# Scores six steps ahead of the weighted latents instead of eight, and a new order of work on every engine

## The chip, the cores and the metric

The kernel runs on one core of one Trainium2 chip. The metric is the device time of one execution in microseconds. A core has five engines that run side by side and synchronise by semaphores: TensorE (PE, matrix products), VectorE (DVE), ScalarE (ACT), GpSimd (POOL) and SyncE (SP), which here issues DMA copies.

## The reference

Input: x of 32 batches x 256 tokens x 128 features, in fp32. Output: x plus an attention term (with its own residual) plus a feed-forward term.

```python
x = L0_attn_x
xn = _layernorm(x)                       # no scale, no bias
# attention, on xn
h = layernorm(xn) * ln_scale + ln_bias
c_q, c_kv = h @ w_down_q.T, h @ w_down_kv.T            # 64 latents each
q, k, v = (c_q @ w_up_q.T), (c_kv @ w_up_k.T), (c_kv @ w_up_v.T)   # 16 heads of 64
q, k = rope(q), rope(k)
attn = softmax(q @ k.T / 8)                            # 256 x 256 per head
att = (attn @ v) @ w_out.T + xn
# feed-forward, on xn
y = square(relu(xn @ W_fc.T)) @ W_proj.T
spikes = 5 steps of a leaky integrator on y, mean of the spikes
return x + att + spikes
```

## The kernel before

**Steps.** The 16 heads of a batch are 8 pairs; one pair of one batch is a step, so there are 256 steps g. The loop body is written for two steps at once (a double step), and a batch b has four of them, q = 0 to 3. Every engine runs the same sequence of double steps, and in each it works on several steps at once, each at another stage. `LEAD` (L27) says how far a stage runs ahead of the last one: at double step g TensorE projects steps g+14 and g+15, POOL finishes the rotation of g+12 and g+13, the scores, maxima, exponentials and transposes are those of g+8 and g+9, and the weighted latents those of g and g+1. The first double step is g = -14 (`FIRST`).

**One step, in order.** `project` (TensorE, L341, L342: four f32r products into the one bank `ps_qk`); `copy_projected` (ACT, L626: raw); `rotate` (DVE, L813: times cosine, which frees `ps_qk` for the next projection); `exchange` (SP, L273: two copies of 128 KB each way swap neighbouring partitions of two steps, `partner`; it waits until POOL is done with the buffer of four steps before, and for raw); `add_rotated` (POOL, L1010 and L1013: times sine, plus); `scores` (TensorE, L353, half the rows of the array for each of two heads); `row_max` (DVE, L818); `exponentials` (ACT, L614: four of them with row sums); `turn` (DVE, L830: 32x32 transposes into `turned`).

**The move.** `move` (SP, L260 to L264) brings the turned weights of a group of four steps into `gathered` by 16 copies of 128 KB. It waits for the last transpose of the group, then for the weighted latents that last read this half of `gathered`. In double step s it is the group whose last step is s + LEAD["scores"] + 1, which falls on q = 1 and q = 3. `weigh_latents` (TensorE, L369, half the columns for each of two heads) waits at the first step of a group for all 16 copies (`moved`). `copy_u` (ACT, L633) takes the result.

**Once per batch.** The sums of the exponentials are inverted (`invert_sums`, DVE L837), split (`split_sums`, POOL), transposed (`transpose_rden`, TensorE L432), broadcast in four chunks (`broadcast_rden`, TensorE L440; `copy_spread`, ACT L639), multiplied in (`normalise_u`, POOL L1054), and `attention_out` (TensorE L474) multiplies by the output weights in four pieces. The latents of batch b+2 are made by `latents` (TensorE L387), `lead_latents` (ACT L670) and `split_latents` (DVE L858), and the first projection of that batch waits for them. `latents_by_token` (L394), `ffn_in` (L410), `relu`, `square`, `ffn_out` (L423), `integrate` (DVE L866, L869), `add_spikes` (L886), `transpose_sum` (L483), `finish` (L897), `moments_of` (DVE L844, L850), `inverse_std` (POOL L1019 to L1028), `normalise` (ACT L655), `residual` (POOL L1036) and `transpose_inputs` (L382) are the rest.

**What sets the order.** The order is written out by hand, in the `step` function of each engine; an engine does what stands there and waits by semaphores. SP's DMA queue is in order too: a copy is issued after those that stand before it. The buffers that tie the engines: one bank for projections, two for score steps (`ps_s`), one for weighted latents (`ps_u`), `ps_b` for sums, broadcasts and attention output, `ps_a` for latents and feed-forward, eight slots of `qk`, two halves of `turned` and of `gathered`.

## Time and profile before

| | us |
|---|---|
| median of 3 runs (1031.68 to 1032.57) | 1032.14 |
| the profiled execution | 1031.75 |
| its span in the trace | 1030.0 |
| PE busy | 990.9 (96%) |
| ACT, DVE, POOL busy | 914.3, 907.0, 895.2 (89, 88, 87%) |
| DMA engines, share of the main queue; bytes of all | 78.8%; 218 MB |

The span runs from the first to the last recorded instruction. A busy PE is one with matmuls in flight; their ends are modelled, so the distance from start to start is what the rows of matmuls are read by. "PEld" is the loading of weights, which lies beside the matmuls. Granted clock 1.00 is the full 2.4 GHz.

### The profile page before, as it was taken

How to read it: one execution, taken by the hardware profiler on the slowest of the kernel's cores; microseconds unless marked ns; L12 is line 12 of the kernel's file. 1: busy time of each engine (PE TensorE's matmuls, PEld its weight loads, DVE VectorE, ACT ScalarE, POOL GpSimd, SP SyncE). 2: the span in 40 equal slices, each digit the busy share in tenths (PEclk: the TensorE clock that was granted, in tenths of full speed). 3: DMA queues.
4: the chain of work that ended last, by engine and by line, in shares of the span. 5: the costliest groups of instructions: out<-in, count | busy, mean ns of one | idle time of the engine just before them, and what ended most of it. 6: DMA issues, size and time to landing. Idle time of an engine off the chain costs nothing.

```text
span 1030.0 us, 25979 instructions
## 1 busy us (share of the span) xinstructions
PE 990.9 (96%) x6880; PEld 732.6 (71%) x6880; DVE 907.0 (88%) x1223; ACT 914.3 (89%) x3007; POOL 895.2 (87%) x898
## 2 busy tenths in 40 slices
PE   4689999999999999999999999999999999999997
PEld 3566777777777777777777777777777777777765
DVE  4898899999999999999999989999999999998972
ACT  4789899999999999999999999999999999999872
POOL 4878989999989999999998999999898999998862
PEclk9899999999999999999999999999999999999999
DMA  6578888888887888888788887888888788888873
GB/s 190 149 215 220 205 220 229 221 216 219 227 211 219 211 217 221 223 215 220 212 217 219 232 206 219 221 208 220 224 216 219 219 210 219 221 211 226 221 184 91
DMA packets 93281, 217.96 MB, mean 212 GB/s; under 512 B 22464, under 2 KB 43200, under 8 KB 93120
## 3 DMA queue, kind: packets, MB, share of 16 engines
q1 hardware_dynamic: 92896, 216.00, 78.8%
q10 hardware_dynamic: 352, 1.57, 0.7%
q8 instruction: 14, 0.23, 0.1%
q14 instruction: 19, 0.16, 0.0%
HBM read 7.77 MB, written 4.19 MB: 12 GB/s over the span
## 4 chain that ended last, share of the span: by engine, by line
PE 80%; issue 6%; DVE 5%; POOL 4%; ACT 2%; SPq 1%; DMA 1%; DVEq 0%; ACTq 0%; POOLq 0%
PE ps_s L353 20%; PE ps_u L369 19%; PE ps_b L474 10%; PE ps_qk L341 7%; PE ps_a L410 5%; PE ps_qk L342 5%; PE ps_a L423 5%; PE ps_b L440 3%; PE ps_a L382 2%; POOL partner L1010 2%; POOL qk L1013 2%; DVE latent L858 1%; ACT prob L614 1%; DVE turned L830 1%; DVE qk L813 1%
## 5 line engine op out<-in xcount | busy, mean ns | idle before, releaser
L614 ACT ACTIVATE prob<-ps_s,neg_max 128x256 f32<-128x256 f32 x1024 | 478.4, 501 | 21.7 <-DVE neg_max L818 19.4
L1010 POOL TENSOR_TENSOR partner<-partner,rope_sb 128x512 f32<-128x512 f32 x256 | 327.4, 1279 | 46.5 <-DMA partner<-raw 46.1
L830 DVE STREAM_TRANSPOSE turned<-prob 128x1024 f32<-128x1024 f32 x256 | 316.8, 1238 | 38.7 <-ACT prob L614 37.3
L1013 POOL TENSOR_TENSOR qk<-qk,partner 128x512 f32<-128x512 f32 x256 | 327.0, 1277 | 20.1
L818 DVE TENSOR_REDUCE neg_max<-ps_s 128x4 f32<-128x1024 f32 x256 | 310.5, 1213 | 18.2 <-PE ps_s L353 13.6
L353 PE MATMUL ps_s<-qk 64*128 64x256 f32 x2048 | 267.6, 395 | 7.1 <-ACT prob L614 4.1
L369 PE MATMUL ps_u<-gathered,ckv 128*64 128x256 f32 x2048 | 249.3, 385 | 1.6 <-DMA gathered<-turned 0.9
L614 ACT ACTIVATION_READ_ACCUMULATOR prob<-ps_s,neg_max 128x1 f32 x1024 | 237.7, 232 | 0.0
L353 PEld LDWEIGHTS ps_s<-qk 64*128 64x128 f32 x2048 | 185.2, 187 | 53.1 <-POOL qk L1013 15.6
L369 PEld LDWEIGHTS ps_u<-gathered,ckv 128*64 128x64 f32 x2048 | 135.6, 136 | 80.5 <-issue 9.9
L813 DVE TENSOR_TENSOR qk<-ps_qk,rope_sb 128x512 f32<-128x512 f32 x246 | 165.4, 672 | 20.9 <-ACT raw L626 19.3
L626 ACT COPY raw<-ps_qk 128x512 f32<-128x512 f32 x246 | 150.5, 612 | 31.8 <-PE ps_qk L342 31.8
L1054 POOL TENSOR_TENSOR u_sb<-u_sb,spread 128x512 f32<-128x512 f32 x124 | 158.8, 1280 | 11.4 <-ACT spread L639 11.4
L341 PE MATMUL ps_qk<-latent,wup_hi 128*128 128x256 f32 x492 | 158.3, 344 | 10.1 <-DVE qk L813 4.6
L341 PEld LDWEIGHTS ps_qk<-latent,wup_hi 128*128 128x128 f32 x492 | 92.5, 188 | 60.5 <-issue 29.6
L342 PE MATMUL ps_qk<-latent,wup_lo 128*128 128x256 f32 x492 | 126.7, 280 | 0.0
L474 PE MATMUL ps_b<-u_sb,wvo_sb 128*128 128x256 f32 x496 | 122.1, 379 | 1.0 <-ACT spread L639 1.0
L474 PEld LDWEIGHTS ps_b<-u_sb,wvo_sb 128*128 128x128 f32 x496 | 89.7, 190 | 11.3 <-ACT spread L639 1.2
L342 PEld LDWEIGHTS ps_qk<-latent,wup_lo 128*128 128x128 f32 x492 | 93.2, 189 | 1.6
L633 ACT COPY u_sb<-ps_u 128x512 f32<-128x512 f32 x128 | 79.4, 620 | 7.5 <-PE ps_u L369 7.4
L639 ACT COPY spread<-ps_b 128x512 f32<-128x512 f32 x124 | 77.1, 621 | 5.4 <-PE ps_b L440 4.2
L410 PE MATMUL ps_a<-xn_t,wfc_sb 128*128 128x256 f32 x256 | 69.9, 396 | 0.0
(85 smaller groups left out, 925.6 us busy)
## 6 DMA issues: line engine op xcount, KB each, us to landing
gathered<-turned SPq DMA_DIRECT2D x1020, 128.0 KB, 2.3
partner<-raw SPq DMA_DIRECT2D x256, 256.0 KB, 2.4
x_sb<-in_x SPq DMA_DIRECT2D x32, 128.0 KB, 2.1
resid<-early SPq DMA_DIRECT2D x32, 128.0 KB, 2.0
out<-out_sb SPq DMA_DIRECT2D x32, 128.0 KB, 2.0
turned<-in_wup ACTq DMA_DIRECT2D x2, 512.0 KB, 6.0
rope_sb<-in_rope SPq DMA_DIRECT2D x1, 512.0 KB, 6.9
turned<-in_wo_t SPq DMA_DIRECT2D x1, 512.0 KB, 7.5
```

The lines of the kernel that those rows point to most:

```text
L341: nc.tensor.matmul(bank, wup_hi[:, which, cols], rhs, start=True, stop=False)
L342: last = nc.tensor.matmul(bank, wup_lo[:, which, cols], rhs, start=False, stop=True)
L353: last = nc.tensor.matmul(ps_s[:, s % 2, h, t, :], qk[rows, s % RING, 0, t * P:(t + 1) * P], qk[rows, s % RING, 1, :], start=True, stop=True)
L369: last = nc.tensor.matmul(ps_u[h * L:(h + 1) * L, j * S:(j + 1) * S], ckv[:, (s // PAIRS) % 2, kt, :], gathered[:, (s // GROUP) % 2, :, (s ...
L474: last = nc.tensor.matmul(ps_b[:, 0:S], wvo_sb[:, pair, :], u_sb[:, par, pair, :], start=(pair == 0), stop=(pair == PAIRS - 1))
L614: last = nc.scalar.activation(prob[:, s % 2, :, h, :, t, :].rearrange("p j k c -> p k j c"), ps_s[:, s % 2, h, t, :].rearrange("p (k j c) ...
L813: nc.vector.tensor_tensor(qk[:, s % RING, :, :], up_bank(g), cos_sb, ALU.mult).then_inc(cos_ready, 1)
L818: nc.vector.tensor_reduce(neg_max[:, s % 2, :, :], ps_s[:, s % 2, :, :, :], AXIS_X, ALU.max, negate=True).then_inc(max_ready, 1)
L830: nc.vector.transpose(turned[:, par, :, s % GROUP, :], prob[:, s % 2, :, :, :, :, :].rearrange("p j h k t c -> p j (h k t c)"))\
L1010: nc.gpsimd.tensor_tensor(other, other, sin_sb, ALU.mult).then_inc(sin_ready, 1)
L1013: nc.gpsimd.tensor_tensor(qk[:, s % RING, :, :], qk[:, s % RING, :, :], other, ALU.add).then_inc(rope_done, 1)
L1054: nc.gpsimd.tensor_tensor(two, two, spread[:, c % 2, :, :], ALU.mult).then_inc(u_norm, 1)
```

## The change

`LEAD` becomes 12, 10 and 6 for projections, rotations and scores. With it the group whose last step is s + 7 falls on q = 0 and q = 2, so the moves stand there, behind the exchange. The order of the calls changes on every engine; no call is added or taken away, and the copies keep their size of 128 KB. The diff, with ACT, DVE and POOL cut to what the prediction speaks of:

(indentation shortened)

```diff
@@ -24,7 +24,7 @@
 LN_EPS = 1e-5
 BETA, THRESHOLD, NUM_STEPS = 0.9, 1.0, 5
 
-LEAD = {"project": 14, "rope": 12, "scores": 8, "multiply": 0}
+LEAD = {"project": 12, "rope": 10, "scores": 6, "multiply": 0}
 RING = 8
 FIRST = -LEAD["project"]
 CHUNKS = PAIRS // 2
@@ -295,6 +295,8 @@
     if q == 0:
         if raws:
             exchange(i * BODY + ahead, ahead)
+        if last % GROUP == GROUP - 1 and not outside(i * BODY + last, STEPS):
+            move(i, last, (0, 1, 2) if isinstance(g, int) and i * BODY + last == STEPS - 1 else (0, 1, 2, 3))
     elif q == 1:
         if not outside(b - 2, B):
             store(b - 2, b0)
@@ -303,19 +305,17 @@
             keep_residual(b0)
         if raws:
             exchange(i * BODY + ahead, ahead)
-        if last % GROUP == GROUP - 1 and not outside(i * BODY + last, STEPS):
-            move(i, last, (0, 1, 2) if isinstance(g, int) and i * BODY + last == STEPS - 1 else (0, 1, 2, 3))
     elif q == 2:
         if raws:
             exchange(i * BODY + ahead, ahead)
+        if last % GROUP == GROUP - 1 and not outside(i * BODY + last, STEPS):
+            move(i, last, (0, 1, 2) if isinstance(g, int) and i * BODY + last == STEPS - 1 else (0, 1, 2, 3))
     else:
         if not outside(b + 2, B) and not outside(b + 4, B):
             sp.wait_ge(res_ready, done(b + 2))
             load_x(b + 4, b0)
         if raws:
             exchange(i * BODY + ahead, ahead)
-        if last % GROUP == GROUP - 1 and not outside(i * BODY + last, STEPS):
-            move(i, last, (0, 1, 2) if isinstance(g, int) and i * BODY + last == STEPS - 1 else (0, 1, 2, 3))
 
 run(sp, prologue, step)
 for b in (B - 2, B - 1):
@@ -521,47 +521,48 @@
             latents(b + 2, b0)
         if projected:
             project(g + far + 1, s + far + 1, i)
+        if not outside(b + 1, B):
+            latents_by_token(b + 1, 1 - b0)
+        if spread:
+            broadcast_rden(b - 1, 0)
         if not outside(g, STEPS):
             weigh_latents(g, s, i)
-        if spread:
-            broadcast_rden(b - 1, 0)
     elif q == 1:
-        if not outside(b + 1, B):
-            latents_by_token(b + 1, 1 - b0)
         if scored:
             scores(g + near, s + near)
             scores(g + near + 1, s + near + 1)
-        if spread:
-            broadcast_rden(b - 1, 1)
         if projected:
             project(g + far, s + far, i)
+        if spread:
+            broadcast_rden(b - 1, 1)
         if not outside(b, B):
             ffn_out(b, 0)
             ffn_out(b, 1)
+        if spread:
+            broadcast_rden(b - 1, 2)
         if projected:
             project(g + far + 1, s + far + 1, i)
-        if spread:
-            broadcast_rden(b - 1, 2)
         if not outside(g, STEPS):
             weigh_latents(g, s, i)
         if is_last(b):
             transpose_last_rden(b)
     elif q == 2:
+        if spread:
+            broadcast_rden(b - 1, 3)
         if scored:
             scores(g + near, s + near)
             scores(g + near + 1, s + near + 1)
         if projected:
             project(g + far, s + far, i)
         if spread:
-            broadcast_rden(b - 1, 3)
+            attention_out(b - 1, 0, 1 - b0)
+            attention_out(b - 1, 1, 1 - b0)
+        if projected:
+            project(g + far + 1, s + far + 1, i)
+        if not outside(b + 1, B):
+            ffn_in(b + 1, 0, 1 - b0)
         if not outside(g, STEPS) and not is_last(b):
             weigh_latents(g, s, i)
-        if projected:
-            project(g + far + 1, s + far + 1, i)
-        if spread:
-            attention_out(b - 1, 0, 1 - b0)
-        if isinstance(b, int) and b == -2:
-            value_by_output()
         if is_last(b):
             broadcast_last_rden(b)
     else:
@@ -570,31 +571,28 @@
             weigh_latents(g, s, i)
             last_attention_out(b, 0, b0)
             last_attention_out(b, 1, b0)
-        if spread:
-            attention_out(b - 1, 1, 1 - b0)
-        if not outside(b + 1, B):
-            ffn_in(b + 1, 0, 1 - b0)
-        if projected:
-            project(g + far, s + far, i)
         if scored:
             scores(g + near, s + near)
             scores(g + near + 1, s + near + 1)
+        if projected:
+            project(g + far, s + far, i)
         if not outside(b + 1, B):
             ffn_in(b + 1, 1, 1 - b0)
+        if not outside(g, STEPS) and not is_last(b):
+            weigh_latents(g, s, i)
         if spread:
             attention_out(b - 1, 2, 1 - b0)
+            attention_out(b - 1, 3, 1 - b0)
         if projected:
             project(g + far + 1, s + far + 1, i)
-        if spread:
-            attention_out(b - 1, 3, 1 - b0)
-        if not outside(g, STEPS) and not is_last(b):
-            weigh_latents(g, s, i)
         if not outside(b + 3, B):
             transpose_inputs(b + 3, 1 - b0)
         if not outside(b - 1, B):
             transpose_sum(b - 1)
         if not outside(b, LAST):
             transpose_rden(b)
+        if isinstance(b, int) and b == -2:
+            value_by_output()
         if is_last(b):
             last_attention_out(b, 2, b0)
 
@@ -724,8 +722,48 @@
     raws, exps = not outside(g + far, STEPS), not outside(g + near, STEPS)
     spread = not outside(b - 1, LAST)
     if q == 0:
+        if not outside(b, B) and not is_last(b):
+            square(b, 1)
         if spread:
             copy_rden(b - 1)
+        if raws:
+            copy_projected(g + far, s + far, i)
+        if exps:
+            exponentials(g + near, s + near, i)
+            exponentials(g + near + 1, s + near + 1, i)
+        if raws:
+            copy_projected(g + far + 1, s + far + 1, i)
+        if not outside(b + 1, B) and not outside(b + 2, B):
+            lead_latents(b + 2, b0)
+        if not outside(g, STEPS):
+            copy_u(g, s, i)
+        if not outside(b + 1, B):
+            copy_latents(b + 1, 1 - b0)
+        if spread:
+            copy_spread(b - 1, 0)
+        if is_last(b):
+            square(b, 1)
+            move_last(3)
+    elif q == 1:
+        if raws:
+            copy_projected(g + far, s + far, i)
+        if spread:
+            copy_spread(b - 1, 1)
+        if exps:
+            exponentials(g + near, s + near, i)
+        if raws:
+            copy_projected(g + far + 1, s + far + 1, i)
+        if spread:
+            copy_spread(b - 1, 2)
+        if exps:
+            exponentials(g + near + 1, s + near + 1, i)
+        if spread:
+            copy_spread(b - 1, 3)
+        if not outside(g, STEPS):
+            copy_u(g, s, i)
+        if is_last(b):
+            copy_last_rden(b)
...
@@ -928,14 +926,13 @@
             rotate(g + far, s + far)
         if turns:
             row_max(g + near + 1, s + near + 1)
+            turn(g + near, s + near, i)
         if not outside(b + 1, B) and not outside(b + 3, B):
             moments_of(b + 3, 1 - b0, i + 1 + b0)
         if turns:
-            turn(g + near, s + near, i)
+            turn(g + near + 1, s + near + 1, i)
         if rotates:
             rotate(g + far + 1, s + far + 1)
-        if turns:
-            turn(g + near + 1, s + near + 1, i)
         if is_last(b):
             invert_sums(b, b0)
@@ -952,16 +949,14 @@
             row_max(g + near + 1, s + near + 1)
         if not outside(b, B):
             integrate(b, b0, 0)
+            integrate(b, b0, 1)
+            integrate(b, b0, 2)
+        if rotates:
+            rotate(g + far + 1, s + far + 1)
+        if not outside(b, B):
+            integrate(b, b0, 3)
         if turns:
             turn(g + near, s + near, i)
-        if not outside(b, B):
-            integrate(b, b0, 1)
-            integrate(b, b0, 2)
-        if not outside(b, LAST):
-            invert_sums(b, b0)
-        if rotates:
-            rotate(g + far + 1, s + far + 1)
-        if turns:
             turn(g + near + 1, s + near + 1, i)
     elif q == 2:
         if turns:
@@ -969,14 +964,15 @@
         if rotates:
             rotate(g + far, s + far)
         if not outside(b, B):
-            integrate(b, b0, 3)
             integrate(b, b0, 4)
         if turns:
             row_max(g + near + 1, s + near + 1)
+            turn(g + near, s + near, i)
         if rotates:
             rotate(g + far + 1, s + far + 1)
+        if not outside(b, LAST):
+            invert_sums(b, b0)
         if turns:
-            turn(g + near, s + near, i)
             turn(g + near + 1, s + near + 1, i)
         if is_last(b):
...
@@ -1068,8 +1064,6 @@
     b = i * UNROLL + b0
     ahead, spread = LEAD["rope"], not outside(b - 1, LAST)
     if q == 0:
-        if not outside(b + 1, B) and not outside(b + 3, B):
-            inverse_std(b + 3)
         if not outside(g + ahead, STEPS):
             add_rotated(g + ahead, s + ahead, i)
         if spread:
@@ -1083,21 +1077,23 @@
             split_sums(b)
         if not outside(g + ahead, STEPS):
             add_rotated(g + ahead, s + ahead, i)
+            add_rotated(g + ahead + 1, s + ahead + 1, i)
+    elif q == 2:
+        if not outside(b + 1, B) and not outside(b + 3, B):
+            inverse_std(b + 3)
         if spread:
             normalise_u(b - 1, 2, 1 - b0)
         if not outside(g + ahead, STEPS):
-            add_rotated(g + ahead + 1, s + ahead + 1, i)
-    elif q == 2:
+            add_rotated(g + ahead, s + ahead, i)
         if spread:
             normalise_u(b - 1, 3, 1 - b0)
-        if not outside(g + ahead, STEPS):
-            add_rotated(g + ahead, s + ahead, i)
-            add_rotated(g + ahead + 1, s + ahead + 1, i)
         if not outside(b, LAST):
             split_sums(b)
+        if not outside(g + ahead, STEPS):
+            add_rotated(g + ahead + 1, s + ahead + 1, i)
+    else:
         if not outside(b + 2, B):
             residual(b + 2, b0, i + 1)
-    else:
         if not outside(g + ahead, STEPS):
             add_rotated(g + ahead, s + ahead, i)
```

Further on ACT: in q = 2 `normalise` of xn comes before `copy_u`, in q = 3 the order is `relu` half 0, `normalise` of z, exponentials, raw copy, `relu` half 1, exponentials, `square` half 0, `copy_u`, raw copy, `copy_inputs`. The last hunk of DVE puts both `row_max` of q = 3 ahead of the rotation. `value_by_output` and its copies, once at the start, move from q = 2 to q = 3.

## Rows read from the trace of the kernel before

**Rows 1.** Page, part 1: engine, busy us, share of the span, instructions.

```profile
PE 990.9 (96%) x6880; PEld 732.6 (71%) x6880; DVE 907.0 (88%) x1223; ACT 914.3 (89%) x3007; POOL 895.2 (87%) x898
```

**Rows 2.** Window, its us, busy PE, PEld, DVE, ACT, POOL; clock; DMA share; GB/s.

```profile
513.90:544.55 30.65, 30.54 (x217) 22.69 (x216) 28.13 (x39) 28.54 (x94) 28.19 (x29) 1.00 0.82 218
```

**Rows 3.** Timeline of PE through one batch: start us, us, engine, line, operation, tiles, count.

```profile
514.30 1.13 PE L353 MATMUL ps_s<-qk 64*128 64x256 f32 x8
...
516.04 1.13 PE L353 MATMUL ps_s<-qk 64*128 64x256 f32 x8
...
517.51 0.41 PE L341 MATMUL ps_qk<-latent,wup_hi 128*128 128x256 f32 x1
...
518.19 1.95 PE L369 MATMUL ps_u<-gathered,ckv 128*64 128x256 f32 x16
520.07 0.51 PE L440 MATMUL ps_b<-rden_t,sel_sb 128*128 128x256 f32 x2
...
522.82 0.51 PE L440 MATMUL ps_b<-rden_t,sel_sb 128*128 128x256 f32 x2
523.44 0.38 PE L341 MATMUL ps_qk<-latent,wup_hi 128*128 128x256 f32 x1
...
531.27 1.95 PE L369 MATMUL ps_u<-gathered,ckv 128*64 128x256 f32 x16
...
533.71 1.89 PE L474 MATMUL ps_b<-u_sb,wvo_sb 128*128 128x256 f32 x8
535.44 1.03 PE L410 MATMUL ps_a<-xn_t,wfc_sb 128*128 128x256 f32 x4
...
544.96 1.13 PE L353 MATMUL ps_s<-qk 64*128 64x256 f32 x8
```

**Rows 4.** Chain of work that ended last, 546 to 559 us: start us, us, what.

```profile
553.63 0.44 DVE latent L858
...
554.19 0.38 PE ps_qk L341
```

**Rows 5.** Timeline of DVE, first double step of the next batch.

```profile
546.23 1.23 DVE L818 TENSOR_REDUCE neg_max<-ps_s 128x4 f32<-128x1024 f32 x1 [0.49 <-PE ps_s L353]
...
551.94 1.22 DVE L830 STREAM_TRANSPOSE turned<-prob 128x1024 f32<-128x1024 f32 x1
```

**Rows 6.** Timeline of ACT, the same stretch: the raw copy and the exponential behind it.

```profile
549.43 0.60 ACT L626 COPY raw<-ps_qk 128x512 f32<-128x512 f32 x1
549.90 0.51 ACT L614 ACTIVATE prob<-ps_s,neg_max 128x256 f32<-128x256 f32 x1
```

**Rows 7.** Timeline of SP's DMA queue, the same stretch and on.

```profile
544.26 1.10 SPq L273 DMA_DIRECT2D partner<-raw  x2
545.54 10.08 SPq L264 DMA_DIRECT2D gathered<-turned  x16
```

**Rows 8.** Chain, 982 to 1004 us: landing of a move's last copy, and its user.

```profile
999.46 2.37 DMA gathered<-turned
...
1001.87 1.95 PE ps_u L369 x16
```

**Rows 9.** Waits: engine, line waited for, us in total, times, longest us.

```profile
POOL partner L1010 <- DMA partner<-raw: 46.1, 34, 4.8
...
PE ps_u L369 <- DMA gathered<-turned: 0.9, 1, 0.9
```

**Rows 10.** Timelines at both ends: the first move, weigh_latents of steps 0 and 252.

```profile
40.17 10.12 SPq L264 DMA_DIRECT2D gathered<-turned  x16
...
58.35 1.95 PE L369 MATMUL ps_u<-gathered,ckv 128*64 128x256 f32 x16
...
1013.83 1.95 PE L369 MATMUL ps_u<-gathered,ckv 128*64 128x256 f32 x16
```

**Rows 11.** Windows in the lead-in, columns as in rows 2.

```profile
30.00:40.00 10.00, 6.05 (x30) 4.54 (x32) 8.28 (x10) 6.47 (x24) 9.39 (x12) 0.71 0.20 79
50.00:60.00 10.00, 6.17 (x46) 4.25 (x46) 8.17 (x12) 8.52 (x33) 5.29 (x5) 1.00 0.77 222
```

More of the change, by code:

```diff
@@ L555, in step @@
                     if spread:
-                        broadcast_rden(b - 1, 3)
+                        broadcast_rden(b - 1, 1)
+                    if not outside(b, B):
+                        ffn_out(b, 0)
+                        ffn_out(b, 1)
+                    if spread:
[5 more added lines that the diff above has]
+                    if is_last(b):
+                        transpose_last_rden(b)
+                elif q == 2:
+                    if spread:
+                        broadcast_rden(b - 1, 3)
+                    if scored:
+                        scores(g + near, s + near)
+                        scores(g + near + 1, s + near + 1)
+                    if projected:
[3 more added lines that the diff above has]
+                        attention_out(b - 1, 1, 1 - b0)
+                    if projected:
+                        project(g + far + 1, s + far + 1, i)
+                    if not outside(b + 1, B):
+                        ffn_in(b + 1, 0, 1 - b0)
                     if not outside(g, STEPS) and not is_last(b):
                         weigh_latents(g, s, i)
-                    if projected:
-                        project(g + far + 1, s + far + 1, i)
-                    if spread:
-                        attention_out(b - 1, 0, 1 - b0)
-                    if isinstance(b, int) and b == -2:
-                        value_by_output()
                     if is_last(b):
@@ L572, in step @@
                         last_attention_out(b, 1, b0)
-                    if spread:
-                        attention_out(b - 1, 1, 1 - b0)
-                    if not outside(b + 1, B):
-                        ffn_in(b + 1, 0, 1 - b0)
-                    if projected:
-                        project(g + far, s + far, i)
                     if scored:
@@ L736, in step @@
                         exponentials(g + near + 1, s + near + 1, i)
[L737 to L742 removed]
+                    if not outside(b + 3, B):
+                        normalise(b + 3, 1 - b0, 0)
                     if not outside(g, STEPS):
                         copy_u(g, s, i)
[L745 to L754 removed]
+                else:
+                    if not outside(b + 1, B):
+                        relu(b + 1, 0)
+                    if not outside(b + 3, B):
+                        normalise(b + 3, 1 - b0, 1)
                     if exps:
@@ L797, in step @@
                         exponentials(g + near + 1, s + near + 1, i)
+                    if not outside(b + 1, B):
+                        square(b + 1, 0)
+                    if not outside(g, STEPS):
+                        copy_u(g, s, i)
                     if raws:
@@ L801, in step @@
                         copy_inputs(b + 3, 1 - b0)
-                    if not outside(g, STEPS):
-                        copy_u(g, s, i)
+                    if isinstance(b, int) and b == -2:
+                        copy_value_by_output()
             run(act, prologue, step)
@@ L986, in step @@
                         row_max(g + near, s + near)
+                        row_max(g + near + 1, s + near + 1)
                     if rotates:
@@ L989, in step @@
                     if turns:
-                        row_max(g + near + 1, s + near + 1)
                         turn(g + near, s + near, i)
```

71 lines of the change are left out of this document (9 added, 62 removed).

## The prediction

> **What bounds the kernel now.** I read the page's busy shares first, then three stretches of one batch each, then the timeline of TensorE through one batch, then the chain of waits, and last the queue that issues the copies between the stages.
>
> TensorE is busy 96% of the span and the others 87 to 89% [rows 1]. In the middle it is busy 30.54 of 30.65 us, one batch, with the clock fully granted [rows 2]. The first score group of a batch starts at 514.30 and that of the next at 544.96 [rows 3]: 30.65 us per batch. So the steady part is TensorE, and only TensorE's order can shorten it. In that order three things are to be seen [rows 3]:
> - Matmuls of the whole array follow each other without loss: attention_out starts at 533.71 and takes eight instructions to 535.44, 0.216 each. A projection is 0.47 (four of 0.117), a broadcast 0.23, latents 0.43, latents_by_token 0.22, two ffn or attention_out pieces 1.73, two score steps 1.73, weigh_latents 1.73.
> - Scores use half the rows and weigh_latents half the columns, and each change of form costs something: from 514.30 to 516.04 one score step and one projection take 1.74, where 0.86 and 0.47 leave 0.41 for two changes; from 517.51 to 520.07 a projection and a weigh_latents take 2.56, where 0.47 and 1.73 leave 0.36 for two. I use 0.20 for a change, and 0.14 for one from a whole-array group into weigh_latents. A batch has 17 changes.
> - One real wait: the broadcast at 522.82 ends its 0.23 at 523.05 and the projection starts at 523.44, 0.39 late. The chain says why: it waits for DVE's split of the new latents [rows 4].
>
> **The change, part by part.** *TensorE's order.* The projection that needs the new latents comes one double step later, so the 0.39 wait goes; what is late next there is nothing, the split is then 7 us early. Counting the new order, the batch has 16 changes of form where it had 17 (the attention_out pieces are paired, but weigh_latents stands alone more often): 0.20 less. No matmul is added or removed. TensorE alone: 30.65 - 0.39 - 0.20 = 30.06 us per batch.
>
> *ACT, DVE, POOL.* Nothing is added. Their busy time is 28.5, 28.1 and 28.2 us in a batch [rows 2], so at 30.06 there is about 1.6 to 2 us for each. Walking the new orders with the durations of the rows (from one start to the next: exponentials 1.81 a step, row_max 1.14, transpose 1.15, rotation 0.60) I find the closest places at 0.1 to 0.3 us: the second score step of the third double step behind the exponentials of the second, and the first projection of a batch behind DVE's last rotation. Bounds: 0 if they all fit, 0.4 us per batch if each of the two is missed by 0.2. I take 0, for the reason of the next part: a longer batch gives all of them room.
>
> *The lead of six, and the moves: this decides.* A move carries four steps of transposed weights in 16 copies, and weigh_latents of the group's first step waits for all 16. Before, the last transpose of a group is done three double steps ahead of its use; with scores 6 ahead it is two. The chain for the group whose second last and last scores stand in the first double step (q = 0) and whose use is at the end of the third (q = 2), counted from the start of that second score step:
>  1. Scores to second transpose: before it is 546.69 to 551.94 + 1.22, that is 6.47 [rows 5]. The new order takes the raw copy from between the two exponentials (0.47 less [rows 6]) but puts the moments between the transposes (about 0.9, of which the rotation's 0.6 is saved and some was idle): transpose done at about 6.3.
>  2. SP issues an exchange first. Its raw copy now follows the exponentials (done at 5.1), two issues of 1.1 in all [rows 7] plus semaphores: the move's first copy starts at 6.6.
>  3. Sixteen issues, 10.08 [rows 7]: 16.7.
>  4. The last copy lands 2.37 after its issue and weigh_latents starts 0.04 later [rows 8]: 19.1.
>
> What TensorE does between that score step and that weigh_latents in the new order: one score step 0.86, latents 0.43, five projections 2.35, latents_by_token 0.22, four broadcasts 0.94, two weigh_latents 3.46, two double score steps 3.46, ffn_out 1.73, two attention_out 1.73, one ffn_in 0.86 = 16.04, and nine changes of form (six of 0.20, three of 0.14) 1.62, in all 17.7. The data come at 19.1: TensorE stands 1.4 us. In a longer batch DVE has a little less queue ahead of row_max, so I take 1.3. Bounds: with no queue anywhere the chain is 1.27 (scores to row_max) + 1.23 + 1.93 + 1.25 + 0.1 + 10.08 + 2.37 = 18.3 [rows 3, 5 to 8], a wait of 0.6; with the exchange held up for a further 0.6 by POOL it is 2.0. The other group (scores in the third double step, used at the end of the next batch's first) has 20.5 of TensorE between and needs about 21.6, 1.1 too little; but the first wait lies inside its stretch and covers it, and likewise the other way. So the batch pays the larger of the two once, not both. Since the scores of the next group come behind the waiting matmuls on TensorE, nothing catches up: it is a loop, and the wait is paid in every batch. Queued behind it are the scores of the last double step, on which DVE and ACT wait. Before, the same copies had 4 us to spare (issued 545.54 to 555.62 [rows 7], landed at 558.0 by the 2.37, used at 531.27 + 30.65 = 561.9 [rows 3]), and the page shows one single wait of this kind, 0.9 us [rows 9].
>
> Period: 30.06 + 1.3 = 31.35 us, 0.7 more than before.
>
> A rule of the Trainium skill speaks against this sum. DMA: Bandwidth & Descriptors, section Anatomy of one DMA, gives a DMA 2.0 us fixed plus its bytes at 436 GB/s (measured there on the path of GpSimd, here SP issues). A move of 16 x 128 KB would then land 6.8 us after its start, the data would be there 4 us before their use, and the first rival below would be the result. The trace disagrees: one move keeps the queue 10.08 us before the landing even begins. The same page's rules say that spreading copies over engines saves only sequencer issue time; here that is exactly what is short.
>
> *Moved issues on SP.* Moves go to the first and third double step, behind an exchange. SP issues 16 + 16 + 8 + 3 copies per batch, 26 us of 31, so it keeps up. The exchange of the fourth double step stands behind a 10.08 us move, and POOL's rotations wait for it: before, POOL waited 46.1 us in all [rows 9], 1.5 per batch. I find the last such rotation done 2.3 us before its scores start. Cost 0; if that cover goes, see the rival.
>
> *Both ends.* The lead-in is one double step shorter. The first move starts at 40.17 [rows 10] because the first four steps' transposes end there, and those stand as early as before; 12.6 later is 52.8, the first weigh_latents, where it was 58.35: 5.5 gained. At the end, the last batches have no projections: 1.9 less in the last period. From weigh_latents of step 248 to that of 252 it was 1001.87 to 1013.83; now the last move starts later against it, second score step + 16.4 (6.3 + 12 copies of 0.63 on SP, four on ACT beside them, + 2.4), which is 13.8 after weigh_latents of step 248, since that one starts 2.6 after the score step. From there to the end the same 16.1 as before (1030.0 - 1013.8).
>
> Sum: 52.8 + 31 x 31.35 - 1.9 + 13.8 + 16.1 = 1052.7 span. The profiled execution lasted 1031.75 for a span of 1030.0, so 1.75 around it: 1054.4, and that execution lies 0.4 under the median of 1032.14, which I leave out: **1054 us**. The two ends may be off by 3 us together.
>
> **Rivals.**
> - *No wait (faster).* The copies land in time and TensorE's new order is all that counts: 52.8 + 31 x 30.06 - 1.9 + 29.9 = 1012.7, + 1.75 = 1014. It decides from the point where a move takes under 11.1 us from its first issue to its use (17.7 - 6.6) where the rows give 12.5. For it: 0.9 us of such waits so far. Against it: issue times are the same in every move.
> - *Bare chain (slower, little).* The wait is 0.7 in place of 1.3 (the 18.3, and 0.1 for the first pair of exponentials in the way): 1054 - 31 x 0.6 = 1036. It needs each engine free at the right moment; DVE has the moments in between.
> - *Two waits.* POOL or SP delays the second group by another 0.5 beyond the first wait: 1054 + 31 x 0.5 = 1070.
> - *POOL becomes the bound.* The exchanges behind the moves come late, as in the lead-in, where POOL stood 3.98 and 4.76 us for one: its 29 us of work and 4 of waiting make a period of 33: 1105. Against: 2.3 us of cover.
> - *The clock.* Each wait might lower TensorE's clock. Where it did (0.71 in 30 to 40 us), TensorE had little to do for 20 us; in 50 to 60 us it stood 3.8 of 10 at full clock [rows 11]. I give it almost nothing.
>
> **How the numbers follow.** Forecast 66% (its own range 1043 to 1064, the wait 0.95 to 1.6), bare chain 8%, two waits 9%, POOL or clock 4%, no wait 8%; 5% that the wait is the bare 0.6 and eats just what the order gives. What a measurement of this kernel can tell from no change is about 0.2%, 2 us. Range 1036 to 1071. Faster 8%, same 5%, slower 66 + 8 + 9 + 4 = 87%.
>
> **What would show it.** Right: weigh_latents waits for gathered once a batch, 1.3 us, some 40 us in all, always in the third double step; the batch period is 31.3; the projection's wait for the latents is gone; each move still takes 10.1 us on SP; the first weigh_latents is near 53. Wrong: a period under 30.65; waits of scores for POOL's sums in place of it; moves that issue faster than 0.63 us a copy.

## The result and the profile after

The changed kernel takes 1047.14 us (median of 4 runs, 1045.50 to 1049.24), the kernel before 1032.04 in the same session: ratio 1.0144, 95% interval 1.013 to 1.0158, 15 us slower. The forecast was 1054 us, slower, with a range of 1036 to 1071. The profiled execution lasted 1048.39 us for a span of 1046.6.

The page's first part, and the window of one batch, answer to [rows 1, 2]:

```profile
PE 995.0 (95%) x6880; PEld 731.1 (70%) x6880; DVE 902.6 (86%) x1223; ACT 917.8 (88%) x3007; POOL 896.0 (86%) x898
```

```profile
516.95:547.80 30.85, 30.77 (x217) 22.77 (x217) 27.86 (x38) 28.68 (x95) 28.19 (x29) 1.00 0.82 216
```

This batch is 0.2 us longer than the 30.65 of [rows 2]; the work, the clock and the transfers are those of before. Neither kernel has a constant period (before it alternates between 30.65 and 30.75, after it lies between 30.75 and 30.91), so from here on "period" is the mean over 21 batches, from the weigh_latents that opens batch 7 to that of batch 28: 30.70 before, 30.82 after.

The waits, answering to [rows 9] (waited for, us in total, times, longest), first of the whole span, then of 230 to 940 us alone:

```profile
POOL partner L1006 <- DMA partner<-raw: 75.2, 40, 9.0
...
PE ps_u L369 <- DMA gathered<-turned: 13.3, 23, 2.8
```

```profile
PE ps_u L369 <- DMA gathered<-turned: 2.1, 11, 0.2
```

weigh_latents does wait for the move, 13.3 us where it was 0.9. But in the 23 batches of the steady part it is 2.1 us; 11.2 lie at the two ends (3.6 before 230 us, 7.7 behind 940). A table by the start of weigh_latents, read from the timeline of TensorE (us), shows where the time is, with the run of 12 copies a move (below) beside it:

| stretch | before | after | 12 copies |
|---|---|---|---|
| start to step 0 | 58.4 | 56.0 | 56.1 |
| to batch 7 | 214.2 | 220.4 | 215.9 |
| to batch 29 (22 batches) | 675.1 | 679.7 | 675.5 |
| to step 248 (two batches) | 54.2 | 61.3 | 57.5 |
| to the end | 28.1 | 29.3 | 29.7 |
| span | 1030.0 | 1046.6 | 1034.7 |

The chain of the move in one batch of after, from the timelines of PE, DVE, SP's queue and PE again (start us, us, engine line):

```profile
520.01 1.13 PE L353 MATMUL ps_s<-qk 64*128 64x256 f32 x8
```

```profile
524.71 1.21 DVE L828 STREAM_TRANSPOSE turned<-prob 128x1024 f32<-128x1024 f32 x1
```

```profile
526.39 10.09 SPq L264 DMA_DIRECT2D gathered<-turned  x16
```

```profile
532.51 2.25 PE L353 MATMUL ps_s<-qk 64*128 64x256 f32 x16
...
538.42 1.95 PE L369 MATMUL ps_u<-gathered,ckv 128*64 128x256 f32 x16
```

Second score step at 520.01, transpose done at 525.92, first copy at 526.39, last issue over at 536.48, weigh_latents at 538.42: 5.9, 6.4, 16.5 and 18.4 us behind the score step, where the prediction had 6.3, 6.6, 16.7 and 19.1. The last copy's issue runs from 535.88 to 536.48 and the copy lands at 538.28. The pair of score steps at 532.51 takes 2.25 where the pair at 524.93 takes 2.00: 0.25 more, in the place that the prediction named as closest, where the score step waits for the exponentials of the double step before.

Both ends. At the start, the first move is issued at 43.83, not at 40.17 [rows 10]; behind it POOL waits 9.0 us once for an exchange that stands behind the first moves. At the end, without projections, TensorE has less to do and waits for the moves:

```profile
1017.33 1.95 PE L369 MATMUL ps_u<-gathered,ckv 128*64 128x256 f32 x16 [2.84 <-DMA gathered<-turned]
...
1031.30 1.95 PE L369 MATMUL ps_u<-gathered,ckv 128*64 128x256 f32 x16 [1.54 <-DMA gathered<-turned]
```

### The profile page after: what moved, and what is told of

The parts are those of the page before. It is cut to its first block, busy times and chain, and to the rows that moved or that the text cites. A ratio compares the mean times of both kernels' runs of the same rounds, so it can differ in the third digit from the quotient of the medians.

```text
span 1046.6 us, 25992 instructions
## 1 busy us (share of the span) xinstructions
PE 995.0 (95%) x6880; PEld 731.1 (70%) x6880; DVE 902.6 (86%) x1223; ACT 917.8 (88%) x3007; POOL 896.0 (86%) x898
## 4 chain that ended last, share of the span: by engine, by line
PE 59%; SPq 10%; POOL 9%; issue 9%; DVE 4%; ACT 4%; DMA 3%; DVEq 0%; POOLq 0%; ACTq 0%
PE ps_u L369 16%; PE ps_s L353 15%; SPq L264 9%; PE ps_b L474 8%; PE ps_qk L341 5%; POOL partner L1006 4%; ACT prob L612 4%; PE ps_a L410 3%; PE ps_qk L342 3%; PE ps_a L423 3%; DMA gathered<-turned 3%; POOL qk L1009 3%; PE ps_b L440 2%; DVE neg_max L816 2%; POOL u_sb L1050 1%
## 5 line engine op out<-in xcount | busy, mean ns | idle before, releaser
L828 DVE STREAM_TRANSPOSE turned<-prob 128x1024 f32<-128x1024 f32 x256 | 313.3, 1233 | 15.0 <-ACT prob L612 10.4
L353 PE MATMUL ps_s<-qk 64*128 64x256 f32 x2048 | 272.0, 397 | 5.3 <-ACT prob L612 3.7
L369 PE MATMUL ps_u<-gathered,ckv 128*64 128x256 f32 x2048 | 250.4, 386 | 16.3 <-DMA gathered<-turned 13.3
L612 ACT ACTIVATION_READ_ACCUMULATOR prob<-ps_s,neg_max 128x1 f32 x1024 | 225.2, 220 | 0.0
L369 PEld LDWEIGHTS ps_u<-gathered,ckv 128*64 128x64 f32 x2048 | 139.9, 137 | 102.0 <-issue 32.7
L341 PE MATMUL ps_qk<-latent,wup_hi 128*128 128x256 f32 x494 | 154.0, 334 | 5.8 <-DVE qk L811 5.8
L410 PE MATMUL ps_a<-xn_t,wfc_sb 128*128 128x256 f32 x256 | 67.0, 385 | 0.0
```

The lines of the kernel that those rows point to most:

```text
L341: nc.tensor.matmul(bank, wup_hi[:, which, cols], rhs, start=True, stop=False)
L353: last = nc.tensor.matmul(ps_s[:, s % 2, h, t, :], qk[rows, s % RING, 0, t * P:(t + 1) * P], qk[rows, s % RING, 1, :], start=True, stop=True)
L369: last = nc.tensor.matmul(ps_u[h * L:(h + 1) * L, j * S:(j + 1) * S], ckv[:, (s // PAIRS) % 2, kt, :], gathered[:, (s // GROUP) % 2, :, (s ...
L612: last = nc.scalar.activation(prob[:, s % 2, :, h, :, t, :].rearrange("p j k c -> p k j c"), ps_s[:, s % 2, h, t, :].rearrange("p (k j c) ...
L828: nc.vector.transpose(turned[:, par, :, s % GROUP, :], prob[:, s % 2, :, :, :, :, :].rearrange("p j h k t c -> p j (h k t c)"))\
```

## The experiments

**The two halves of the change, each alone.** order8: the new order with `LEAD` 14, 12, 8 and the moves in q = 1 and 3.

```diff
-LEAD = {"project": 12, "rope": 10, "scores": 6, "multiply": 0}
+LEAD = {"project": 14, "rope": 12, "scores": 8, "multiply": 0}
```

> The new order on every engine with the old leads of 14, 12 and 8; the moves go back to q = 1 and q = 3, and value_by_output to q = 2. Theory M (the changed kernel is bound by the loop scores, transposes, 16 copies, weighted latents, which the lead of six makes too short): with one more double step between a move and its use the wait is gone and only the order is left, 0.6 us less per batch than before: 1012 to 1020 us. Rival O (the new order itself costs, by ACT, DVE or POOL running short at a lower period, or by exchanges that stand behind the moves): 1030 us or more.

Measured: 1077.8 us, ratio 1.0417 (1.040 to 1.0435), period 32.08. Theory M's 1012 to 1020 us falls: freed of the move's wait, the new order gains nothing. Its timeline and its waits show one place: the first projection of the new latents falls in q = 1 again when the leads are 14, and in the new order fewer of TensorE's calls of q = 1 stand in front of it (`latents_by_token` is in q = 0, a broadcast behind it).

```profile
545.70 0.38 PE L341 MATMUL ps_qk<-latent,wup_hi 128*128 128x256 f32 x1 [1.12 <-DVE latent L856]
```

```profile
PE ps_qk L341 <- DVE latent L856: 34.4, 30, 1.4
```

lead6: the old order with the leads 12, 10, 6 and the moves in q = 0 and 2 (ACT's `normalise` one double step later).

> The old order on every engine with the new leads of 12, 10 and 6; moves at q = 0 and q = 2, value_by_output at q = 3, and normalise one double step later, since the shorter lead-in would leave it out. Theory M: between the second score step of q = 0 and the weigh_latents of q = 2 stand 15.2 us of TensorE where the chain takes 18.4, a wait of 3.2 us in each batch: 1110 to 1130 us. Rival O: the lead costs little, 1025 to 1045 us.

Measured: 1221.1 us, ratio 1.1808 (1.1785 to 1.1832), some 100 us above what M expected; period 36.4, a granted clock of 0.941 over the run.

```profile
PE ps_u L369 <- DMA gathered<-turned: 133.8, 60, 4.7
```

Twice a batch the move comes too late. Order alone costs 1.4 us a batch, leads alone 5.7, the two together 0.12: neither half can be judged by itself.

**The size of the move.** copies12: three of four rows of blocks are moved after the first two groups; the rest of `gathered` keeps the weights of those groups, and the four copies that ACT issues in the last move are left out too.

```diff
-move(i, last, (0, 1, 2) if isinstance(g, int) and i * BODY + last == STEPS - 1 else (0, 1, 2, 3))
+move(i, last, (0, 1, 2, 3) if isinstance(g, int) and i * BODY + last < 2 * GROUP else (0, 1, 2))
```

> The changed kernel with 12 instead of 16 copies in each move after the first two; a quarter of the transposed weights is not moved and weigh_latents reads old ones. Theory M: the chain is 2.5 us shorter, above the 0.75 us of waiting that it causes, so the period falls to TensorE's own 30.1 to 30.3 and the end is nearer too: 1018 to 1028 us. Rival O: 1040 us or more, since order and other engines stay.

Measured: 1036.3 us, ratio 1.0032 (1.0016 to 1.0047), period 30.71, no wait for gathered between 230 and 940 us. The copies cost the changed kernel 10.8 us (11.9 in span), but the time stops 8 us above what I had expected: with the move out of the way the new order's period is that of the old one. By the table, 4.2 of the 11.9 us lie in the 22 steady batches, 4.5 before batch 7 and 3.8 in the two periods before step 248.

copies18: two more copies of 128 KB a move, into a tile that nothing reads.

```diff
+for block_of in range(2):
+    sp.dma_start(aside[32 * block_of:32 * block_of + 32, par, :], turned[0:32, par, block_of, :, :]...).then_inc(moved[par], 16)
```

> The changed kernel with two more copies of 128 KB in each move, into a tile that nobody reads. Theory M: each batch is longer by the whole of their issue time, 1.27 us: about 40 us more, 1080 to 1092 us. Rival O: the issues lie in SP's idle time, under 1057 us.

Measured: 1089.8 us, ratio 1.0539 (1.0501 to 1.0577), period 32.04, as expected.

```profile
PE ps_u L374 <- DMA aside<-turned: 55.1, 58, 4.4
```

Two copies are 1.27 us of issuing, and the period rises by 1.21: once a batch, not twice. TensorE does wait at both groups, though. By the distances between the starts of its matmuls, means over 18 batches, 1.05 of the 1.21 us stand at the weigh_latents of q = 2 and 0.26 at that of q = 0, with 0.10 less at a score step. The loop of the move and the order of TensorE are nearly tied in the changed kernel: 12 copies give 30.71, 16 give 30.82, 18 give 32.04. Taking the 1.27 off again puts the loop at 30.77, an estimate. Of the same means, 16 copies against 12 add 0.20 us at q = 0 and 0.10 at q = 2 and take 0.18 off the waits for the other engines: net 0.12.

b_18copies: the same two copies in the kernel before.

> The kernel before with two further copies of 128 KB in each move, into a tile that nothing reads; the first weighted latents of a group wait for all 18. The same addition cost the changed kernel 42.7 us (1089.8 against 1047.1). Theory M (slack under the lead of eight): there the last copy lands 3.9 us ahead of its use, 1.27 more leaves 2.6, and the time is at most 1036 us, with next to no wait of TensorE for the move. Rival Q (the queue of SP is the bound whatever the lead, and delays exchanges and POOL): the two copies cost 1.27 us twice a batch or more here too, 1060 us or more, with POOL waiting for the exchange longer than 46 us in all.

Measured: 1053.3 us, ratio 1.0187 (1.0162 to 1.0213), between the two theories. The period is 30.98, only 0.28 more for 2.54 us of further issuing, and no wait of TensorE for the move is among its rows; so the slack under a lead of eight is real, as in theory M. But 9.2 us of the 22 in span come before batch 7, and SP's queue is felt elsewhere, as Q had it:

```profile
POOL partner L1015 <- DMA partner<-raw: 79.2, 51, 6.2
...
PE ps_s L358 <- POOL qk L1018: 10.0, 19, 2.7
```

**TensorE alone.** The next three kernels leave work out, to see how long a batch is when TensorE waits for nobody: exponentials, row_max and the product with the sine are done on half of the columns, TensorE's work and order are untouched.

```diff
-prob[:, s % 2, :, h, :, t, :]..., ps_s[:, s % 2, h, t, :]..., ACT.Exp
+prob[:, s % 2, :, h, 0, t, :],    ps_s[:, s % 2, h, t, 0:S // 2]..., ACT.Exp
-nc.vector.tensor_reduce(neg_max[...], ps_s[:, s % 2, :, :, :], ...)
+nc.vector.tensor_reduce(neg_max[...], ps_s[:, s % 2, :, :, 0:S // 2], ...)
-nc.gpsimd.tensor_tensor(other, other, sin_sb, ALU.mult)
+nc.gpsimd.tensor_tensor(other[:, :, 0:S // 2], other[:, :, 0:S // 2], sin_sb[:, :, 0:S // 2], ALU.mult)
```

a12_light is copies12 with it:

> The changed kernel with 12 of the 16 copies of a move after the first two (1036.3 us, 30.71 per batch), and with ACT, DVE and POOL made lighter: exponentials and row_max work on half of the columns, POOL's product with the sine too, about 3.5, 4.4 and 5 us less per batch. TensorE's work and order are unchanged. It measures my first term, TensorE alone in the new order. Theory T: the 30.06 us are right, and the 0.65 us above them are small waits for ACT and DVE; the period is 30.0 to 30.2 and the time 1013 to 1020 us. Rival U: I counted the changes of form wrongly and the new order costs TensorE 30.6 by itself; period 30.5 or more, 1029 us or more.

b_light is the kernel before with it:

> The kernel before with the same lighter work of ACT, DVE and POOL (exponentials, row_max and the product with the sine on half of the columns). It measures TensorE alone in the old order. By my sum the 0.39 us wait for the latents goes, since DVE reaches the split earlier, and one more change of form (0.20) than in the new order stays: period 30.26, 1019 us (1016 to 1022), 0.2 us per batch above the lighter changed kernel. Rival: both orders are the same to TensorE, and the periods of the two lighter kernels agree within 0.05; second rival: the old order has waits of another kind and stays at 30.6 or more.

Measured: a12_light 1022.0 us (ratio 0.9892, 0.9876 to 0.9909), b_light 1020.7 us (0.9886, 0.9868 to 0.9905). One batch of each, first the new order, then the old:

```profile
510.52:540.86 30.34, 30.33 (x216) 22.46 (x214) 23.96 (x39) 25.35 (x95) 23.81 (x29) 1.00 0.67 186
```

```profile
510.76:541.14 30.38, 30.38 (x216) 22.59 (x216) 23.78 (x39) 25.52 (x94) 23.67 (x28) 1.00 0.84 221
```

Neither theory of a12_light holds as put: TensorE's own period is 30.33, between the 30.06 of the sum and the 30.5 of the rival. For b_light the first rival is right: the two orders, 30.33 and 30.38, are the same to TensorE within 0.05.

a16_light: the changed kernel with all 16 copies and the lighter engines.

> The changed kernel with all 16 copies in its moves, and with the lighter ACT, DVE and POOL of the 1022.0 us run (exponentials, row_max and the product with the sine on half of the columns). Scores to move is shorter by some 1.2 us in it (row_max 0.55 and four to eight exponentials of 0.1 each), the move itself is not. Theory M (the move chain is a loop beside TensorE's): the chain of 18.4 us falls to 17.2, below the distance that TensorE's own work gives; no wait for gathered in the steady part, period 30.33 to 30.4 and 1020 to 1026 us, so that the copies cost 4 us or less where they cost the full kernel 10.8. Rival Q: the wait for gathered is set by SP's queue (26 us of issues in 30.3) and stays, period 30.6 or more, 1031 us or more.

Measured: 1030.5 us (median of 10 runs, 1026.8 to 1035.8), ratio 0.9984 (0.9967 to 1.0001). The period is 30.34, with one wait for gathered of 0.5 us between 230 and 940 us: in the steady part theory M holds, since SP issues as much in this kernel as in the full one and is no bound. M's price for the copies was too low, though: 1030.5 against the 1022.0 of a12_light is 8.5 us, where M had 4 or less. Only 0.9 of it lies in the 22 steady batches; the rest is at the ends, where TensorE still waits for moves:

```profile
1012.43 1.95 PE L369 MATMUL ps_u<-gathered,ckv 128*64 128x256 f32 x16 [1.68 <-DMA gathered<-turned]
```

**The wait for the latents.** Four tries to take the one real wait of the old order [rows 4] away, or to mend order8 by it. b_split: the split in q = 0, ahead of the second transpose (in this diff and the next the conditions around the calls are left out).

```diff
 elif q == 0:
+    split_latents(b + 2, b0)
     turn(g + near + 1, s + near + 1, i)
 elif q == 1:
-    split_latents(b + 2, b0)
     row_max(g + near, s + near)
```

> The kernel before with one call moved: DVE splits the latents of batch b+2 in the first double step of a batch, ahead of its second transpose, instead of at the start of the second. TensorE's order and the leads are those of before. Theory L (my second term of TensorE's order): the first projection of a batch waits 0.39 us for the split and nothing else is late, so the wait goes, the period falls from 30.70 to 30.3 and the time is 1031.8 - 31 x 0.39 = 1020 us (1018 to 1024), with no row of PE waiting for the latents. Rival R (the order is loose only on paper): the split's 0.4 us on DVE come ahead of a transpose and of the row maxima behind it, another wait of TensorE takes the place of this one within the batch, as the changed kernel's small waits did, and the time is 1028 to 1034 us, with the wait for latents gone all the same.

Measured: 1050.2 us, ratio 1.0165 (1.0152 to 1.0179), worse than either theory. The wait is gone and a larger one is there, at the second projection of q = 1: DVE stands for ACT's copies of the latents, and TensorE behind DVE's rotation:

```profile
562.46 0.86 DVE L858 TENSOR_TENSOR latent<-ps_a,latent 64x256 fp32r<-64x256 f32 x2 [0.77 <-ACT ckv L675]
```

```profile
566.50 0.38 PE L341 MATMUL ps_qk<-latent,wup_hi 128*128 128x256 f32 x1 [0.59 <-DVE qk L813]
```

o8_split: order8 with the rotation and the split ahead of the second transpose in q = 0.

> The new order with the old leads of 14, 12 and 8 (1077.8 us, 32.08 per batch), with DVE's split of the latents moved up to the first double step, between the rotation and the second transpose. Theory L: what made the new order slow at the old leads was the first projection of a batch, which again waited 1.12 us for the split in every batch; taken away it leaves 1077.8 - 31 x 1.15 = 1042 us or less, 1030 to 1044, period 30.7 to 31.0. Rival R: the wait is the sign of a loop through DVE, ACT and POOL that the leads set (the order was drawn for stages two steps later), it shows up under another name, and the time stays at 1060 us or more.

Measured: 1079.1 us, ratio 1.0447 (1.0431 to 1.0463), period 32.07. Rival R. The split waits for ACT's copies in the same way (DVE latent behind ACT ckv, 21.7 us in all) and the projection still waits 24.9 us for it. Whether the wait for latents is the loop of order8 or its sign stays open.

b_split2: b_split, and ACT's two latent copies ahead of the second step's exponentials.

```diff
+lead_latents(b + 2, b0)
+copy_latents(b + 1, 1 - b0)
 exponentials(g + near + 1, s + near + 1, i)
-lead_latents(b + 2, b0)
-copy_latents(b + 1, 1 - b0)
```

> The kernel before with two calls moved in the first double step of a batch: DVE splits the latents of batch b+2 ahead of its second transpose (as in the run that took 1050.2 us), and ACT copies the latents out ahead of the second step's four exponentials instead of behind them. In the 1050.2 us run DVE stood 0.77 us at the split for ACT's copies (562.46, its last copy starting at 562.16), and row_max, rotation and projection behind it came late. Theory L2: the 0.39 us wait of TensorE is real, and my first cure failed only because ACT delivered late; with ACT's copies 1.8 us earlier DVE does the same work without a gap, all behind it stays in its place, the period falls from 30.70 to 30.3 and the time to 1020 us (1017 to 1025). Rival R: any reordering here is given back: the exponentials that now come 1.0 us later hold up the second transpose or the raw copy of the next projection, and the time is 1029 us or more.

Measured: 1135.2 us, ratio 1.0988 (1.0971 to 1.1006), period 34.16. The copy of the latents also waits for `latents_by_token` of the batch before, which TensorE only does in q = 1 (L394). ACT stood in front of the exponentials, and TensorE behind them. The timelines of ACT and of PE, and the granted clock behind it, in two windows of the 5 us that follow and in one inside them (columns as in [rows 2]):

```profile
574.51 0.75 ACT L670 CAST latent<-ps_a 64x256 fp32r<-64x256 f32 x2 [1.90 <-PE ps_a L394]
```

```profile
577.53 1.24 PE L353 MATMUL ps_s<-qk 64*128 64x256 f32 x8 [2.04 <-ACT prob L614]
```

```profile
577.53:580.14 2.61, 2.61 (x14) 2.18 (x15) 2.36 (x2) 1.89 (x4) 2.39 (x3) 0.67 0.88 234
580.14:582.52 2.38, 2.38 (x9) 1.95 (x9) 1.45 (x2) 2.11 (x9) 2.30 (x3) 0.64 0.70 239
...
578.50:581.80 3.30, 3.30 (x12) 2.79 (x11) 2.11 (x4) 2.31 (x7) 3.22 (x3) 0.50 0.89 283
```

b_split3: b_split2, and TensorE's `latents_by_token(b + 1)` directly behind `latents(b + 2)`.

> The run of 1135.2 us with one call more moved: TensorE's latents_by_token of batch b+1 goes from the start of the second double step to right behind latents in the first. In the 1135.2 us run ACT's copy of the latents stood 1.90 us for that very product (574.51), because it also waits for the batch before; the exponentials behind it came late and TensorE's second score step waited 2.04 us for them. Theory L3: with the product early ACT and DVE run without a gap, and the only remaining question is whether the second step's exponentials, 1.0 us later than before, are still in time for the second score step of the next double step. Before, they end at 551.86 and that score step starts at about 552.5, so 0.4 of the 1.0 is missing: the wait for latents (0.33 net) is exchanged for one of about the same size, period 30.6 to 30.8, 1028 to 1036 us. Rival L: the full gain, 30.35, 1020 to 1024 us. Rival R: a loop as in the two runs before, 1045 us or more.

Measured: 1034.5 us (median of 11 runs, against 1032.6 of the kernel before), ratio 1.0023 (1.0014 to 1.0032), period 30.79: theory L3. The wait for latents has become a wait for exponentials, once a batch:

```profile
556.63 1.13 PE L353 MATMUL ps_s<-qk 64*128 64x256 f32 x8 [0.19 <-ACT prob L614]
```

Here the exchange is visible: from start to start the wait at the projection is gone and the score step is 0.34 us late (means over 18 batches), so the 0.33 us were moved, not taken away. No version beats the kernel before.

## Why the prediction came out as it did

It had the sign, and a time 7 us too high; that it came so near is partly luck. It put nearly all of the loss into 31 equal batches, 0.7 us each. Measured, a steady batch lost 0.12, and most of the 16.6 us of span came before batch 7 and in the last periods. Three terms of the period were mis-sized, and their errors cancelled in part.

| term | predicted | measured |
|---|---|---|
| TensorE alone, new order | 30.06 | 30.33 |
| ACT, DVE, POOL | 0 (0 to 0.4) | 0.38 (30.71 - 30.33) |
| wait for the move | 1.3 | 0.11 (30.82 - 30.71) |
| period | 31.35 | 30.82 |
| first weigh_latents | 52.8 | 56.0 |
| step 0 to step 248 | 969.95 | 961.3 |
| step 248 to 252, 252 to the end | 13.8 + 16.1 | 14.0 + 15.3 |
| around the span | 1.75 | 1.8 |

*TensorE's order.* The changes of form are 16 against 17 as counted, but the sum overrated them. From 30.70 (I used the shorter of the two alternating periods, 30.65) the new order sheds 0.33 for the wait, net of what stands at such a place anyway, and only 0.04 for the rest, by the two lighter kernels (30.70 - 0.33 - 0.04 = 30.33). The 0.16 missing come back in small gaps between groups, the largest 0.11, in front of the broadcast that now follows latents_by_token.

*Cost 0 for the other engines* was the step that failed most clearly. The reason given was that a longer batch would give them room; it wasn't long enough. The place named first did come true (the score steps of q = 2, 0.22 us in copies12 against a12_light), the second did not show; another 0.13 stand at ffn_out, which was not foreseen, and what is left is under 0.04 at any place.

*The chain of the move.* Its mechanism stands: issue time of 16 copies, 10.09 us, decides; 1.27 more makes the period 1.21 longer; it falls away with 12 copies. Its size does not. Predicted, 19.1 us of chain stood against 17.7 of TensorE. Measured, the chain is 18.4 to 18.5. It has 0.4 less on DVE, and the sum counted 0.59 us twice: the 2.37 of [rows 8] runs from the start of the last issue, not from its end, as the same chain of the kernel before shows. The issue before it is over at 999.42, and 999.46 is where the last one starts:

```profile
998.83 0.59 SPq L264
999.42 0.04 issue
```

So the last issue is in the 10.08 and in the 2.37. In the changed kernel the last copy lands 1.80 behind the end of its issue and weigh_latents starts 0.14 later. Without the double count the predicted chain would have been 18.5, and the slack before the change 4.5 us rather than 4. On the other side of the comparison, the distance on TensorE from second score step to weigh_latents is 18.0 in a12_light and 18.4 in copies12, where the small waits of the last paragraph are in it. 19.1 - 17.7 became 18.5 - 18.4. The "bare chain" rival (18.3, 1036 us) came near the length by luck, as its sum has the same 0.59 in it twice, and the "no wait" rival had the loss of the wait, but both added them to a TensorE of 30.06 that no run shows. That only the third double step waits did not hold either: in the changed kernel q = 0 waits 0.20 and q = 2 0.10.

*The copies' price.* Each move keeps the queue for 10.09 us, as before. The 2.0 us plus bytes at 436 GB/s that the Trainium skill gives for GpSimd's path (DMA: Bandwidth & Descriptors, section Anatomy of one DMA) would have given no wait, which is near the 0.11 us of the steady part, but for another reason: by that formula a move is an estimated 6.8 us, and the trace after has 11.9 from the first issue to the last landing (526.39 to 538.28). The landings do not wait for the end of the issuing, as the prediction has it: the first copy of this move lands at 528.69.

*Ends.* The 5.5 us at the start became 2.3, as the first four steps' transposes end 3.7 later than I assumed; which engine's new order delays them I haven't followed. The first seven batches take 4.6 us more than seven steady periods, and only with 16 copies (0.9 with 12). In that stretch POOL waits 29 us for exchanges, against 16 with 12 copies, and TensorE waits for moves too (3.6 us); so the fourth rival may hold for some batches, but no run separates the two. The last periods cost more too: I took 1.9 off for the missing projections, but there TensorE waits 7.7 us for moves. So the 16.6 us of span are -2.3 at the start, +6.1 to batch 7, +4.5 in the 22 batches, +7.1 in the two before step 248 and +1.2 behind, rather than 0.7 in every batch.

*The clock.* The fifth rival was rightly given little: the steady batches of the changed kernel run at 1.00. Its reading of the lead-in was loose: in the 20 us in which it says that TensorE had little to do, TensorE was busy 7.15 and 6.05 of 10 us. And waits of 2 us did lower the clock in b_split2 (below).

Of the signs listed, "each move takes 10.1 us" and "the wait for latents is gone" were seen; "a wait once a batch, 1.3 us, 40 in all" was not (0.2 or less, 13.3 in all), nor were 31.3 and 53.

## What to carry to other kernels

When the engines behind the bound stand at 90%, a gap that is taken from the bound's order can come back under another name, as here in copies12 and b_split3; make the other engines lighter in an experiment to see what the order alone is worth before counting on it. For a loop beside the bound (score, transpose, move, use), both its length and the distance it must fit into carry an error of half a microsecond, so the difference of the two is known to a microsecond at best, and the range should say so. Where one duration is added to another, check from which event each is counted: a landing time that runs from the start of an issue already holds that issue. Look at the first and last batches by themselves, since a price per batch times their number missed most of this loss. Before moving a copy ahead, read everything that it waits for, also what belongs to the batch before.

## What the runs showed of the hardware

- A wait of 2 us can cost TensorE nearly twice that. In b_split2 it stood 2.04 us in a batch; over the 5.0 us behind that the granted clock was 0.67 and 0.64 on average, and from 578.5 to 581.8 it was 0.50, which is the lower level, 1.2 GHz: a projection's matmuls started 0.21 us apart instead of 0.12. A third of 5.0 us is an estimated 1.7 more, and 30.38 + 2.04 + 1.7 = 34.1 is near the 34.16 of the period. Over the whole run the clock was 0.949, in lead6, with waits of up to 4.7 us, 0.941, in copies18 0.984; in b_split, with 0.59 us, it was 0.995 as in the kernel before. Not every such wait does it: in the last batch of the changed kernel TensorE stood 2.84 us up to 1017.33, and the granted clock was 1.00 from 1010 to 1036.
- SP issues a copy of 128 KB between partitions every 0.63 us, in every kernel here. It lands 2.35 us behind the start of its issue (the median), 1.8 behind its end. Two further copies a move, 1.27 us of issuing, cost 1.21 a batch where weigh_latents waits for them (copies18) and 0.28 where it does not (b_18copies), with more waiting of POOL for exchanges (79.2 us against 46.1).
